# A three-layer CIN tower on one core: the last batch step of 64 rows becomes two of 32, GpSimd's gathers are dealt out anew, and filler matmuls are added

## The reference, cut to what matters

```python
# B = 1024, M = 32 fields, D = 16; e: gathered rows, one of each table
e = jnp.stack([tbl_f[ids[:, f]] for f in range(32)], axis=1)      # 1024 x 32 x 16
x0, xk, outs = e, e, []
for W in (W0, W1, W2):                                             # W: 32 x H x 64
    xk = relu(einsum('bmd,bhd,mhk->bkd', x0, xk, W))
    outs.append(xk.sum(axis=2))
h = concatenate(outs + [dense_ctx], axis=1)                        # 1024 x 208
h = relu(h @ W_top1 + b_top1); h = relu(h @ W_top2 + b_top2)       # 512, then 256
y = h @ W_top3                                                     # 1024 x 1
```

## Time and profile before

| | us |
|---|---|
| median of 3 timed runs | 613.42 |
| lowest and highest | 612.62, 616.33 |
| the profiled execution's own time | 615.86 |
| its span in the profile | 614.0 |
| TensorE busy in it | 570.6 |
| VectorE busy in it | 551.8 |
| GpSimd busy in it | 478.9 |

### The profile page before, as it was taken

The page is one execution under the profiler, slowest core; times in us unless marked ns, Lnnn a source line. Parts: engine busy times, 40 slices in busy tenths (PEclk is TensorE's granted clock), DMA queues, the critical chain, the costliest instruction groups (busy, mean ns, idle before and its releaser), DMA issues.

```text
span 614.0 us, 8076 instructions
## 1 busy us (share of the span) xinstructions
PE 570.6 (93%) x2706; PEld 206.6 (34%) x2706; DVE 551.8 (90%) x343; ACT 309.7 (50%) x1363; POOL 478.9 (78%) x363
## 2 busy tenths in 40 slices
PE   0599887999999989999999999999999999999997
PEld 0244422322323323333333333333332333343344
DVE  0199969999999999999999999999999999999490
ACT  0144716454546746454555747454555746453542
POOL 6766688868888878989888888888887898939260
PEclk9899998999999999999999999999999999999997
DMA  3696848676977767677878667677777667676000
GB/s 100 241 364 264 341 155 317 230 293 257 350 279 284 283 220 269 231 278 257 315 278 310 252 235 273 221 270 277 300 278 302 208 240 303 231 291 230 1 1 0
DMA packets 34788, 150.89 MB, mean 246 GB/s; under 512 B 7830, under 2 KB 15578, under 8 KB 18362
## 3 DMA queue, kind: packets, MB, share of 16 engines
q1 hardware_dynamic: 26544, 148.26, 62.9%
q0 software_dynamic: 8192, 2.11, 3.0%
q10 hardware_dynamic: 10, 0.00, 0.0%
HBM read 147.20 MB, written 3.15 MB: 245 GB/s over the span
## 4 chain that ended last, share of the span: by engine, by line
PE 51%; POOL 16%; DVE 12%; DMA 10%; issue 9%; ACT 1%; SPq 1%; DVEq 0%; POOLq 0%
PE y_ps L568 47%; DVE prod L386 12%; POOL emb L342 10%; DMA x0bc<-x_rows 8%; POOL pool_prod L356 6%; PE x0g_ps L634 2%; DMA emb<-table,row_sb 1%; PE x0g_ps L628 1%; DVE z L414 1%; PE x0g_ps L629 1%; DMA x_rows<-emb 1%; PE x0g_ps L657 1%; PE x0g_ps L639 0%; DMA off_sb<-id_offset 0%; ACT x_ps L468 0%
## 5 line engine op out<-in xcount | busy, mean ns | idle before, releaser
L386 DVE TENSOR_TENSOR prod<-x0bc,x_ps 128x2048 f32<-128x2048 f32 (+2 forms) x270 | 462.1, 1779 | 13.9 <-ACT x_ps L468 12.8
L568 PE MATMUL y_ps<-prod,w_sb 128*64 128x512 f32 (+1 forms) x1772 | 383.8, 567 | 9.6 <-DVE prod L386 8.8
L342 POOL DMA_INDIRECT emb<-table,row_sb x256 | 244.8, 956 | 71.0 <-issue 69.0
L356 POOL TENSOR_TENSOR pool_prod<-x0bc,x_sb 128x1024 f32<-128x1024 f32 (+1 forms) x101 | 233.2, 2317 | 44.3 <-ACT x_sb L485 36.7
L568 PEld LDWEIGHTS y_ps<-prod,w_sb 128*64 128x64 f32 x1772 | 123.5, 137 | 245.7 <-issue 208.9
L475 ACT ACTIVATE relu<-y_ps 128x16 f32<-128x16 f32 x480 | 79.6, 291 | 113.4 <-PE y_ps L568 113.4
L468 ACT ACTIVATE x_ps<-y_ps 64x512 f32<-64x512 f32 (+1 forms) x136 | 74.1, 545 | 111.1 <-PE y_ps L568 108.4
L568 PE MATMUL y_ps<-pool_prod,w_sb 128*64 128x512 f32 (+1 forms) x404 | 101.7, 583 | 5.0 <-POOL pool_prod L356 4.9
L386 DVE TENSOR_TENSOR prod<-x0bc,x0g_ps 128x2048 f32<-128x2048 f32 (+1 forms) x34 | 72.1, 2153 | 24.4 <-DMA x0bc<-x_rows 22.6
L485 ACT ACTIVATE x_sb<-relu 64x512 f32<-64x512 f32 (+1 forms) x128 | 78.8, 615 | 3.4
L475 ACT ACTIVATION_READ_ACCUMULATOR relu<-y_ps 128x1 f32 x480 | 79.8, 318 | 0.1
(11 more groups left out here) (36 smaller groups left out, 81.1 us busy)
## 6 DMA issues: line engine op xcount, KB each, us to landing
x0bc<-x_rows SPq DMA_DIRECT2D x128, 1024.0 KB, 7.6
x0g<-x_rows SPq DMA_DIRECT2D x15, 512.0 KB
emb<-table,row_sb POOLq DMA_INDIRECT x256
x_rows<-emb SPq DMA_DIRECT2D x15, 128.0 KB
x_rows<-emb SPq DMA_DIRECT2D x17, 64.0 KB
w_sb<-w SPq DMA_DIRECT2D x2, 512.0 KB, 4.6
x0g<-x_rows SPq DMA_DIRECT2D x2, 256.0 KB
wt_sb<-wt SPq DMA_DIRECT2D x1, 512.0 KB, 4.8
```

Of the source, the lines that this page charges most:

```text
L342: pool.indirect_dma_start(emb[:, turn, DIM * n:DIM * (n + 1)], None, table, bass.IndirectOffsetOnAxis(row_sb[:, at:at + 1], 0)).then_inc(g ...
L356: pool.tensor_tensor(pool_prod[:, n % POOL_RING, 0:width(s)], x0bc[:, tile_columns(s, j)], x[:, 0:width(s)], ALU.mult).then_inc(pool_produ ...
L386: made = dve.tensor_tensor(out, left, right, ALU.mult)
L568: made = pe.matmul(ps[MAPS * h:MAPS * (h + 1), 0:half(s)], w, moving[:, half(s) * h:half(s) * (h + 1)], start=first, stop=final)
```

## The change

The last step of 64 rows becomes two of 32, so that there are 18 steps, 0 to 17. The next to last chunk of the MLP has 224 rows instead of 192, and the last one has 32 instead of 64. Of the two new last steps GpSimd makes 5 and 4 tiles in the first, and 4 and 4 in the second. The gathers are dealt out anew over the start, steps 1 and 2. `keep_going` gets two more matmuls at the start, and one new call between the two halves of the last chunk's first layer.

```diff
-ROWS_OF = [32, 32] + [64] * 15
+ROWS_OF = [32, 32] + [64] * 14 + [32, 32]
...
-POOL_OF = {0: (0, 0), 2: (2, 3), STEPS - 2: (5, 4), STEPS - 1: (5, 4)}
+POOL_OF = {0: (0, 0), 2: (2, 3), STEPS - 3: (5, 4), STEPS - 2: (5, 4), STEPS - 1: (4, 4)}
...
-GATHERED_FIRST = 32
+GATHERED_FIRST = 34
 GATHERS_AFTER = {1: [1, 1, 8], 2: [1, 1, 4]}
-MORE_GATHERS = {(1, 1): [0, 0, 6], (1, 2): [0, 0, 10], (2, 1): [0, 11], (2, 2): [1, 1, 5]}
+MORE_GATHERS = {(1, 1): [0, 0, 10], (1, 2): [0, 0, 4], (2, 1): [1, 11], (2, 2): [1, 1, 3]}
...
-CHUNKS = [(0, 5), (5, 9), (9, 13), (13, 16), (16, 17)]
+CHUNKS = [(0, 5), (5, 9), (9, 13), (13, 17), (17, 18)]
...
+
+                pe.wait_ge(relu_done[1], STEPS)
+                keep_going((LAST, 1), 1)
                 pe.wait_ge(zt_last, 2)
...
-            keep_going((0, 0), 3)
+            keep_going((0, 0), 5)
             layer0(0)
```

## The result

| | us |
|---|---|
| the change, median of 7 runs | 609.91 (608.41 to 612.34) |
| the kernel before, median of 7 runs on the same chip | 615.51 (612.62 to 616.33) |
| ratio | 0.9926, 95% interval 0.9901 to 0.9951 |
| profiled execution of the change, and its span | 608.41, 606.6 |

The change is 0.7% faster on this chip. The profiled execution is the quickest of its seven, and its span is 7.4 us shorter than that of before, where the medians differ by 5.6 us. So some 1.8 us of what the two traces show apart belongs to these two executions. The clock granted to TensorE, as a mean over the execution, is 0.999 in this trace and 0.994 to 0.998 in the other six executions of the change; it is 0.989 in the trace of before.

The account below looks back on a forecast made before the run. TensorE, VectorE and GpSimd were near the bound together, so gains lay at the two ends: −6.3 + 1.4 − 0.1 − 0.9 − 0.1 = −6.0 us, median 613.4 to 607.4 us (±1.5, chance 0.55), range 604.5 to 611.0.

Parts of the forecast that it names:

- (c): Rival: every step's store 1.25 us late, its load behind VectorE in 12 steps; +7.9 us, 621.3 us; chance 0.05.
- (b): Rival: the end loses, VectorE's 3 us for smaller groups not covered, clock gives nothing; −1.9 us, 611.5 us; chance 0.12.
- Gathers, −6.3: Start: earlier gathers in GpSimd's waits remove VectorE's two holes before step 3, 5.78 and 0.56 us; −6.3 us.
- so store and loads also move by 7.5 us: Step 3's start: the 48th gather ends 7.5 us earlier, and SyncE's store and the loads follow by as much.
- (d): Rival: step 3's hole only moves, ring space or `x0g` being late; a 3 us hole left gives 610.4 us; chance 0.06.
- The late gather, +1.4 (0 to 15): From step 3 on: one gather stands a place later, stores come 1.25 us later; +1.4 us, between 0 and 15.
- There all 1.25 us become a wait of VectorE: Step 12: the later store's whole 1.25 us becomes VectorE's wait, charged 1.0 us as TensorE has work in hand.
- (a): Rival: the late gather costs nothing and the clock stays up; −8.2 us, 605.2 us; chance 0.22.
- Two steps of 32 rows, −0.1: End up to the last tile: TensorE −1.0 + 1.2 + 0.6 − 0.9 = −0.1 us, VectorE's extra 3 us covered by its lead.
- The tail, −0.9 (0 to −1.7): Behind the last tile: half the columns and a filler matmul; gain 0 to 1.7 us from the clock, half taken.
- What it may buy is the clock: Tail: the filler may keep TensorE at 2.4 GHz, L657's 16 records taking 2.1 us instead of 3.61.
- The start, −0.1: Start: two more filler matmuls may prevent the half clock at 27.8 to 31.2 us; 0 to −0.85, taken as −0.1 us.

Follow-up runs that it names:

- the gathers alone: The new deal of the gathers over steps 1 and 2 only, against the kernel before; 637.33 us, ratio 1.0032 (0.9994 to 1.0070).
- the split alone: Last step of 64 rows made two of 32, old gathers, no added fillers, against the kernel before; 633.99 us, ratio 0.9986 (0.9958 to 1.0013).

## Why the prediction came out as it did

The forecast was 607.4 us with a range of 604.5 to 611.0; 609.9 us is inside. It said 1.0% where 0.7% came. It left open whether the gain would reach 1%, with 0.49 for and 0.46 against, and it did not.

**The sum.** That the total came so near is in part luck. The forecast took 6.0 us off; the medians differ by 5.6 and the two traces by 7.4. In the traces the gathers brought 2.3 us less than said. Against that stand 4.1 us in the middle and 1.0 in the tail that came better than said, most of both from things in which executions of one kernel differ (below); the two steps of 32 rows were 1.1 us dearer. The base moved as well: the 613.4 us were a median of three, and over seven the kernel before takes 615.5, from which the same 6 us would give 609.5. Two slips are in the sums of the rivals: with its own terms (c) has −7.4 and not −7.1, so 621.0 us, and the 611.5 of (b) lies outside the range as a whole, not by its outer part. By the forecast's own terms:

**Gathers, −6.3.** Right mechanism, wrong size: −4.0 from step 2 to 3, and the two holes are 2.2 us and not 0. The step that failed is "so store and loads also move by 7.5 us". They moved by 4.3 and 3.7 us. It took the gather's landing at what it was in the earlier trace rows, although the new place lies under step 2's loads; the landing grew by 2.4 us. A further 0.8 us went because the added gathers were not quite covered: GpSimd's tile at 64.28 us came at 65.05, behind one at 48.93 instead of 47.62. The last 0.6 us were lost between store and load (1.49 us for the two stores instead of 0.86). On the later chips, in the change, VectorE's layer 0 of step 2 is 29.1 us later than on the first and step 3's store only 27.1 us (104.55 and 77.43), which gives the load the 2 us that it lacked: the holes all but go (0.28 + 0.47 us with the gathers alone, 0.49 in the change), and all seven traces have 28 us from step 2 to 3. That the new deal takes the hole away is shown by itself there: 28.3 us with the gathers alone, 33.0 to 34.0 with the old ones. A wait of 2.2 us left is near rival (d), which put 3 us on it but for another reason (ring space).

**The late gather, +1.4 (0 to 15).** The step "There all 1.25 us become a wait of VectorE" failed on the first chip, where the change has no wait for a load in these steps. Steps 4 to 15 took 379.7 to 380.5 us with the late gather and 380.3 to 380.8 without, on the later chips. VectorE sets their length: it is 377.8 us in the trace without any idle time of VectorE, and on the later chips 1.9 to 2.9 us longer, of which VectorE's idle time is 1.3 to 2.4. What it waits for changed. Waits of at least 0.15 us in front of layer 0 add up to 0 to 1.2 us in the five traces with the old deal and to 1.2 to 2.4 us in the six one place late, about 1.0 us more in the mean, so a price near the one charged is there. But every trace with the old deal also waits 1.1 to 2.1 us for `x_ps`, and none of the six does; the sum had no term for that, and why these waits went is not shown. One place more raises the waits in front of layer 0 to 5.2 us. So the slack that the prediction read off step 7 was the right thing to look at, and its bound was at work one place further on. Rival (a) had the total of this part right. The −2.7 us of the first chip's middle have no counterpart in the later traces. They are the waits of before (1.0 us in front of step 12's layer 0, 1.2 for `x_ps`) and small delays, and as far as these traces tell mostly chance of the two executions.

**Two steps of 32 rows, −0.1.** The end up to E costs +1.0 us on the first chip, and +0.9 to +1.6 in the nine split kernels later (96.7 to 97.3 us against 95.7 to 95.8). The idle 0.99 us did go. From the mark at which TensorE begins the squares of step 16 to E its busy time rose from 57.6 to 59.7 us: L628 and L629 take 3.2 instead of 2.9 us and L634 3.29 instead of 2.87, and the rest is spread over handovers that now come twice as often (the first pair of layer 0 and squares takes 2.3, the second 2.8 us; one of 64 rows took 4.4). That VectorE's extra time is covered was right, and the Trainium skill's rule (VectorE: DVE Perf Modes, "The TRN2 errata") fits the busy time (+1.2 us for 18 more instructions) and decides nothing here. Rival (b) is not what happened: the bound that lost time was TensorE.

**The tail, −0.9 (0 to −1.7).** −1.9 us on the first chip. The cost of the filler was judged rightly: TensorE reaches the second half 2.0 us behind E in the change, where 1.84 was said, and 1.4 us without the filler (622.49 and 621.08 us in the split alone). What failed is the step "What it may buy is the clock". Length of the tail by the clock granted in it, one execution each:

| tail | granted clock: us from E to the end |
|---|---|
| 64 rows, no filler | 0.68: 9.7 (before, first chip); 0.69: 9.6; 0.82: 8.2 |
| 64 rows, filler | 0.81: 8.4 |
| 32 rows, no filler | 0.75: 7.9; 0.80: 7.5; 0.90: 7.2 |
| 32 rows, filler | 0.69: 9.4; 0.72: 9.1 and 9.1; 0.76: 8.7; 0.84: 7.9; 0.92: 7.8 and 7.8 (one of them the change, first chip) |

The clock falls as far with the filler (0.69) as without it (0.68), and stays up about as long (0.92 and 0.90). At like clocks the halved columns alone gain about 0.8 us (8.2 and 7.5), and the filler takes 0.6 to 0.8 us of it back with 32 rows (7.2 and 7.8; 7.9 and 8.7). An estimate from this table for the first chip's −1.9: −0.3 for the new tail at the same low clock (9.7 and 9.4), and −1.6 because the clock of that one execution stayed up, where before's had fallen. The worth of the clock was sized well (1.7 us), and that the first chip's trace got all of it is luck; the filler did not bring it about.

**The start, −0.1.** The clock kept up at 27.8 to 31.2 us, VectorE began 1.1 us earlier at step 0's layer 1 and had lost it at step 1 (+0.3 us). As argued. Here the fillers do what they were for: of the eight traces with five of them none has a half clock between 25 and 31 us, of the six with three of them five have.

**The slower side.** Rival (c) gave a loss through late stores. On the later chips the change did lose 1.3%, but not by (c): steps 4 to 15 are no longer. The loss is ahead of step 4, in matmuls and signals of TensorE that come late, beside or behind series of gathers. Nothing in the first chip's trace showed it, and no rival had it.

## What to carry to other kernels

When an indirect gather is moved to an earlier place, read what the DMA engines do at its new place before moving its landing along: here 2.4 of 6.7 us of earlier issue were lost that way. An instruction that stands one place late may cost nothing in sum and the next place some 4 us, as here; try both places, and sum the waits by what they are for, since one kind can grow while another goes. A filler matmul on the path of a short tail costs its time (0.6 to 0.8 us here), whether the clock stays up or not. A change that fills the last idle time of an engine at the start should be timed on more than one chip: this one was 0.7% faster on one and 1.3% slower on another.

## What the runs showed that I had not expected

The kernel before takes 615.5 us on one chip and 633 to 635 on the others, with nearly the same busy times (TensorE 570.6 and 573.4, VectorE 551.8 and 552.3). Nearly all of the difference lies in front of step 1: 39.7 against 53.9 us in the traces of the kernel before, and up to 62.6 in others. ScalarE's first copy of `x_ps`, of the change on the first chip, of the kernel before and of the change on the later ones:

```profile
28.57 1.50 ACT L468 ACTIVATE x_ps<-y_ps 64x256 f32<-64x256 f32 x4 [6.77 <-PE y_ps L568]
```

```profile
40.05 1.50 ACT L468 ACTIVATE x_ps<-y_ps 64x256 f32<-64x256 f32 x4 [17.94 <-remote]
```

```profile
52.30 1.50 ACT L468 ACTIVATE x_ps<-y_ps 64x256 f32<-64x256 f32 x4 [30.50 <-remote]
```

By its records TensorE had done the products that it waits for by 28 to 29 us in all three (and went on to its fillers, next in its list, at 27.8 to 28.9). The copy comes at 40 to 50 us in the five traces with the old gathers, at 42 and 48 in two with the new ones and at 52 to 53 in the other five. Each of these copies comes while, or a few us after, GpSimd issues its first 32 or 34 gathers, which last until about 44.3 and 46.7 us.

The traces also record when the counter that these copies wait for was raised, which no view prints. It was raised at 52.28, 40.03 and 125.21 us, 0.02 us before the copies at 52.30 and 40.05 us above and the one at 125.23 us, and as short before nearly every such copy on these chips. So ScalarE is not late. The records of the matmuls that raise it end at 28.0, 29.1 and 118.6 us; on the first chip record and signal are 0.03 us apart (28.51 and 28.54). What is late is TensorE's signal, or the real end of its matmuls, since the ends in the profile are modelled. Together with the matmuls that come one by one this says that on these chips something delays TensorE's instructions or its signals near long series of gathers. One caution: these traces lack some of the counter's updates (they have 235 of 270 in the kernel before and 246 of 284 in the change), and the first chip's lack none.

Full DMA engines are not the common ground (0.09 at one of the places, 1.02 from 35 to 45 us), and pacing the tile loads did not help. Whether it is the fetch of TensorE's instructions, the delivery of the signal, or how the chip is set up, stays open: no kernel here moved the gathers off the start, which would have told.
